# Softmax shift rows with the logarithm of the row sum in an attention and feed-forward kernel

## The reference

```
def xattn(q, k, v, wq, wk, wv, wo_w, wo_b):      # q = layernorm(x), k = v = ctx
    qp = rope(q @ wq.T); kp = rope(k @ wk.T); vp = v @ wv.T
    ...                                          # 16 heads of 32 features, blocks of 128 queries
    scores = (qh @ kband.T) * sqrt(32)           # keys at a distance of at most 128, others masked
    attn = softmax(scores)
    return (attn @ vband) @ wo_w.T + wo_b
x = x + xattn(layernorm(x), ctx, ctx, ...)
x = x + ffn(layernorm(x), ...)                   # 512 -> 2048 -> gelu -> 512, int8 weights, 16-bit activations
```

## Time and profile before

| What | Value |
|---|---|
| median of 3 runs | 1174.8 us (1173.72 to 1175.84) |
| the profiled execution's own time | 1176.49 us |
| its span | 1174.8 us |
| busy share: TensorE, VectorE, ScalarE, GpSimd | 97%, 81%, 55%, 32% |
| mean granted clock of TensorE | 0.988 |

### The profile page before, as it was taken

The page is one execution under the profiler, slowest core; times in us unless marked ns, Lnnn a source line. Parts: engine busy times, 40 slices in busy tenths (PEclk is TensorE's granted clock), DMA queues, the critical chain, the costliest instruction groups (busy, mean ns, idle before and its releaser), DMA issues.

```text
span 1174.8 us, 23540 instructions
## 1 busy us (share of the span) xinstructions
PE 1135.5 (97%) x7928; PEld 766.9 (65%) x7928; DVE 946.8 (81%) x2413; ACT 646.8 (55%) x1033; POOL 375.7 (32%) x540
## 2 busy tenths in 40 slices
PE   6999999999999999999999789999999999999998
PEld 6867887887788788778878464444444444444443
DVE  6879989999999999999998756666666687777776
ACT  5255356436534643563464255555555577777774
POOL 1247337534743663474365230000000021111121
PEclk9989999999999999999999799999999999999999
DMA  8554674566457556646753723555553402676662
GB/s 281 133 150 114 172 221 118 148 184 163 126 175 212 129 137 184 172 123 179 203 139 92 222 65 118 197 196 198 196 196 117 152 1 77 214 232 227 224 216 99
DMA packets 100522, 191.10 MB, mean 163 GB/s; under 512 B 13376, under 2 KB 30912, under 8 KB 100416
## 3 DMA queue, kind: packets, MB, share of 16 engines
q1 hardware_dynamic: 96096, 179.92, 50.9%
q10 hardware_dynamic: 4320, 9.83, 2.8%
HBM read 89.16 MB, written 43.91 MB: 113 GB/s over the span
## 4 chain that ended last, share of the span: by engine, by line
PE 44%; DVE 26%; issue 25%; DMA 2%; ACT 1%; SPq 1%; DVEq 0%; POOL 0%; POOLq 0%; ACTq 0%
PE bank L864 19%; DVE bank L1224 12%; PE bank L642 6%; PE bank L656 5%; PE bank L669 5%; DVE row_max L1224 3%; PE bank L589 3%; PE bank L593 2%; DVE neg_max L1265 2%; DVE roped L1250 2%; DVE rt L1248 2%; DVE rt L1247 1%; DVE neg_max L1229 1%; DVE t_lo L1257 1%; PE bank L608 1%
## 5 line engine op out<-in xcount | busy, mean ns | idle before, releaser
L1224 DVE CUSTOM_DVE_ANT_0 bank<-bank,mask 128x256 f32<-128x256 f32 x512 | 203.5, 453 | 33.9 <-PE bank L608 23.1
L864 PE MATMUL bank<-wout_int,g_hi 128*128 128x512 bf16 x512 | 193.6, 379 | 0.1
L864 PE MATMUL bank<-wout_int,g_lo 128*128 128x512 bf16 x512 | 193.6, 379 | 0.0
L825 PE MATMUL bank<-qT_hi,win_int 128*128 128x512 bf16 x496 | 188.0, 379 | 0.0
L825 PE MATMUL bank<-qT_lo,win_int 128*128 128x512 bf16 x496 | 188.0, 379 | 0.0
L973 ACT ACTIVATE probs<-bank 128x512 f32<-128x512 f32 x256 | 139.0, 599 | 37.0 <-PE bank L642 31.1
L1542 POOL TENSOR_TENSOR k_lo<-roped,k_hi 128x256 fp32r<-128x256 f32 x60 | 55.0, 947 | 263.5 <-ACT k_hi L913 263.5
L1520 DVE TENSOR_TENSOR g_lo<-h_int,g_hi 128x512 f16<-128x512 f32 x128 | 89.1, 696 | 41.3 <-ACT g_hi L1129 37.4
L1565 POOL TENSOR_SCALAR_AFFINE_SELECT probs<-probs 128x256 f32<-128x256 f32 x256 | 107.1, 429 | 35.9 <-ACT probs L973 30.0
L1097 ACT ACTIVATE h_ring<-bank,b_in,g_scale 128x512 f32<-128x512 f32 x96 | 73.1, 779 | 71.2 <-PE bank L825 56.4
L1462 DVE TENSOR_REDUCE hmax<-h_ring 128x512 f32 (+1 forms) x96 | 63.1, 682 | 58.5 <-ACT h_ring L1097 56.4
(11 more groups left out here) (170 smaller groups left out, 2735.0 us busy)
## 6 DMA issues: line engine op xcount, KB each, us to landing
hidden_scratch<-h_ring SPq DMA_DIRECT2D x96, 256.0 KB, 2.1
h_ring<-hidden_scratch SPq DMA_DIRECT2D x96, 256.0 KB, 2.9
k_st<-k_hi SPq DMA_DIRECT2D x128, 128.0 KB, 2.9
q_st<-q_hi SPq DMA_DIRECT2D x128, 128.0 KB, 2.7
xq<-x_scratch SPq DMA_DIRECT2D x16, 1024.0 KB, 6.0
x_ln<-in_x SPq DMA_DIRECT2D x16, 512.0 KB, 6.3
ctx_raw<-in_ctxT SPq DMA_DIRECT2D x16, 512.0 KB, 5.0
k_st<-k_lo SPq DMA_DIRECT2D x64, 128.0 KB, 2.8
```

Source lines behind the costliest of these rows:

```text
L825: mm = pe.matmul(bank[f % 4][:], win_int[:, c, f * P:(f + 1) * P], part[:, par, c], start=c == 0 and part is qT_hi, stop=c == KC - 1 and p ...
L864: return pe.matmul(bank[4 * par + u][:], part[:, f % 4, u * P:(u + 1) * P], wout_int[:, f], start=f == 0 and part is g_hi, stop=f == FC - ...
L1224: dve.tensor_tensor_reduce(sc, sc, mask[:, (1 - qb) * P:(1 - qb) * P + S], 1.0, NEG, ALU.add, ALU.max, row_max[:, qb, n:n + 1]).then_inc(m ...
```

## The change

The mask is now 0 or the largest float, the queries' weights are scaled by minus the square root of 32, and VectorE takes row minima of the negated scores (`row_minima`, same two passes). Then ScalarE takes exp(minimum - score) of each half in place in PSUM with `accum_out`, which gives the row sum (`row_sums`, 32 instructions a block). A bank of `ring` is released by ScalarE (`sum_done`) and no longer by VectorE. When all heads are through, `logs` takes the logarithm of the sums and exp of minus that; VectorE's `log_sums` makes of it, in five small chained operations, the shift row (logarithm minus minimum, with one correction step), in two parts. With this row the second set of exponentials is already divided by the sum. So `denominators`, `invert`, `store_sums`, `spread_shares`, `normalise`, `last_shares` and the two constant tables are gone. The transposed row is in bank 6 where it was in bank 7. ScalarE's copies of the first part are placed between its row sums (`xt_lead` behind head 3, `v_copy` behind 8, `split_hi` of the keys behind 9, `ot_lead` behind 12), `ctx_hi` moves behind exponential 4, and GpSimd's four `ctx_lo` move behind the bands of heads 10 to 13. The counts of output products become 12 ahead of the transposes, 4 behind them and 8 among the heads.

```diff
             def scores(b, n):
...
-                    pe.wait_ge(max_done, 2 * (H * b + n - 1))
+                    pe.wait_ge(sum_done, 2 * (H * b + n - 1))
...
             def clump(b, par, i, has_proj):
                 for kb in range(2):
-                    weighted(b, par, i, kb)
-                for kb in range(2):
-                    denominators(b, i, kb, has_proj)
+                    weighted(b, par, i, kb, has_proj)
...
-                some(7)
+                some(12)
                 max_transposes(b, has_proj)
                 some(4)
-                for n, count in enumerate((1, 2, 2, 2, 1, 1, 1, 0, 1, 1, 0, 0, 1, 0, 0, 0)):
+                for n, count in enumerate((1, 1, 1, 1, 1, 0, 1, 0, 1, 0, 0, 0, 1, 0, 0, 0)):
...
+            def row_sums(b, n):
+                if n == 0:
+                    wait(act, lse_chain, LSE_OPS * b)
+                act.wait_ge(min_done, 2 * (H * b + n + 1))
+                for qb in range(2):
+                    sc = ring[n % 2][:, qb * S:(qb + 1) * S]
+                    act.activation(sc, sc, ACT.Exp, scale=-1.0, bias=row_min[:, qb, n:n + 1],
+                                   accum_out=row_sum[:, qb, n:n + 1]).then_inc(sum_done, 1)
+
+            def logs(b):
+                act.wait_ge(sum_done, 2 * H * (b + 1))
+                act.activation(lse[:], row_sum[:], ACT.Ln).then_inc(log_done, 1)
+                act.wait_ge(log_done, 2 * b + 1)
+                act.activation(lse_e[:], lse[:], ACT.Exp, scale=-1.0).then_inc(log_done, 1)
...
             def step(b, par, has_c, has_o, has_proj, has_xt):
                 if has_proj:
                     norm1(b + 1)
-                if has_proj:
-                    xt_lead(b + 1, 0)
-                    xt_lead(b + 1, 1)
-                if has_o:
-                    store_sums(b - 1)
-                    spread_shares(b - 1)
-                if has_proj:
-                    v_copy(b + 1, 1 - par, 0)
-                    split_hi("k", b + 1)
-                if has_o:
-                    ot_lead(b - 1, 0, has_proj)
-                    ot_lead(b - 1, 1, has_proj)
+                for n in range(H):
+                    row_sums(b, n)
+                    if n == 3 and has_proj:
+                        xt_lead(b + 1, 0)
+                        xt_lead(b + 1, 1)
+                    if n == 8 and has_proj:
+                        v_copy(b + 1, 1 - par, 0)
+                    if n == 9 and has_proj:
+                        split_hi("k", b + 1)
+                    if n == 12 and has_o:
+                        ot_lead(b - 1, 0, has_proj)
+                        ot_lead(b - 1, 1, has_proj)
+                logs(b)
                 if has_proj:
                     v_copy(b + 1, 1 - par, 1)
-                if has_xt:
-                    ctx_hi(b + 2)
...
                 for n in range(H):
                     softmax_exp(b, n)
+                    if n == 4 and has_xt:
+                        ctx_hi(b + 2)
...
+            def log_sums(b):
+                hi, lo = shift[:, :, MROW:MROW + H], shift[:, :, MROW + H:P]
+                link = chain(dve, lse_chain, LSE_OPS * b)
+                dve.wait_ge(log_done, 2 * b + 1)
+                link(dve.tensor_tensor(lse_z[:], lse[:], row_min[:], ALU.subtract))
+                dve.wait_ge(log_done, 2 * b + 2)
+                link(dve.tensor_tensor(lse_t[:], row_sum[:], lse_e[:], ALU.mult))
+                link(dve.scalar_tensor_tensor(out=lse_z[:], in0=lse_t[:], scalar=-1.0, in1=lse_z[:], op0=ALU.add, op1=ALU.add))
+                link(dve.tensor_copy(hi.bitcast(F32R), lse_z[:]))
+                link(dve.tensor_tensor(lo.bitcast(F32R), lse_z[:], hi, ALU.subtract))
...
-                    between[0] += [lambda: invert(b - 1)]
-                    between[4] += [lambda: normalise(b - 1, 0), lambda: normalise(b - 1, 1)]
...
-                if has_xt:
-                    ctx_lo(b + 2, 0)
-                    ctx_lo(b + 2, 1)
                 for n in range(H):
                     band(b, n)
                     if 6 <= n < 10 and has_proj:
                         split_lo("q", b + 1, n - 6)
-                    if n in (1, 3) and has_xt:
-                        ctx_lo(b + 2, n // 2 + 2)
+                    if 10 <= n < 14 and has_xt:
+                        ctx_lo(b + 2, n - 10)
```

More of the change, by code:

```diff
@@ L40 @@
 SLOTS = 8
-HOT = DK + NC4 - 1
 FC = FF // P
@@ L74, in constants @@
     q, k = np.arange(S)[:, None], np.arange(S)[None, :]
-    mask = folded(folded(np.where(np.abs(q - k) <= WINDOW, 0.0, NEG).astype(np.float32), 0), 1)
+    mask = folded(folded(np.where(np.abs(q - k) <= WINDOW, 0.0, FAR).astype(np.float32), 0), 1)
     assert not mask[:P, :P].any() and not mask[P:, P:].any()
     mask = np.concatenate([mask[P:], mask[:P, P:]], 1)
-    hot = np.tile((np.arange(HOT) % NC4 == NC4 - 1).astype(np.float32), (P, 1))
-    row, col = np.arange(P)[:, None], np.arange(P)[None, :]
-    pick = np.stack([row == DK * (col // DK) + i for i in range(NC4)], 1).astype(np.float32)
     sel = np.zeros((P, H), np.float32)
@@ L761, in _ @@
             steps(pe, step)
-            def last_shares():
-                pe.wait_ge(pick_in, 16)
-                pe.wait_ge(exp_done, H * NB)
-                for s in range(2):
-                    pe.wait_ge(den_done, NB + s)
-                    for i in range(NC4):
-                        mm = pe.matmul(ring[s][:, i * P:(i + 1) * P], pick[:, i], den_r[:, s * P:(s + 1) * P],
-                                       start=True, stop=True)
-                    mm.then_inc(share_mm, 1)
             def last_products():
@@ L945, in ot_lead @@
             def ot_lead(j, s, has_q):
-                act.wait_ge(onorm, 2 * (j + 1) if j < NB - 1 else 2 * j + s + 1)
+                act.wait_ge(oT_out, 2 * (j + 1))
+                if s == 0:
+                    wait(act, o_mm, 2 * j)
                 if s == 0 and has_q:
@@ L1261, in xt_rest @@
                 rest(x_bank, s, xt_hi, 2 * j + s + 1, xt_lo)
-            def invert(b):
-                dve.wait_ge(den_mm, NC4 * (b + 1))
-                dve.reciprocal(den_r, den_bank[:, 0:S]).then_inc(den_done, 1)
-            def normalise(b, half):
-                dve.wait_ge(oT_out, 2 * b + half + 1)
-                dve.wait_ge(share_in, 16 * (b + 1))
-                part = oT[:, 2 * half:2 * half + 2].rearrange("p i t -> p (i t)")
-                dve.tensor_tensor(part, part, share[:, 2 * half * S:2 * (half + 1) * S], ALU.mult).then_inc(onorm, 1)
             def quantise_win(b):
@@ L1351, in step @@
                             work()
-                split_max(b)
+                log_sums(b)
                 if not has_proj:
```

120 lines of the change are left out of this document (43 added, 77 removed).

## The result

The changed kernel took 1327.1 us (median of 4 runs, 1321.97 to 1329.87) where the kernel before took 1175.3: a ratio of 1.129 (95% interval 1.125 to 1.133). The prediction was 1330. The profiled execution took 1321.97 us, the shortest of the four, with a span of 1320.3, at a mean granted clock of 0.951 (0.988 before).

The account below looks back on a forecast made before the run. TensorE's queue was taken to bound the attention part, ScalarE being half free. First part +8.8 us and second +1.3 made +10.2 a period, +153 for 15 blocks, +5 and -3: 1330 us, range 1260 to 1370.

Parts of the forecast that it names:

- The sum: Whole kernel: period 51.0 us against 40.8; +153 us for 15 blocks, +5 for the last, -3 behind it.
- the walk: Attention part, three engine queues followed in time: first part 33.1 us (+8.8), second 17.9 (+1.3).
- 0.60 us for a half: First part, one ScalarE row sum: 0.41 us exponential and 0.19 us accumulator read; bounds 0.47 to 0.63.
- The rival of the clock: Attention part: TensorE's clock falls after idle stretches, 5 us at 0.6 per block; up to +30 us, 1360; chance 0.08.
- its lower case, 1288: Whole kernel: same walk with row sum 0.47 us and copy 0.19 us; period 48.2 us, time 1288.
- the forecast case: Whole kernel: the walk's 51.0 us period, 1330 us, with no fall of the clock; chance 0.70.
- The signs: Expected in the profile: period near 51 us, TensorE idle 25%, late minima 4, GpSimd full from band 6 to 15.
- the lap of a bank: First part: scores now wait for VectorE and 1.2 us of ScalarE; a bank's lap goes from 1.67 to 2.92 us.
- Rival A: Attention part: ScalarE's content, not the laps, sets a period of 41.8 us; +15 us, 1190; chance 0.10.
- The copy to float32r: Shift row on VectorE: this copy taken as 0.6 us, between 0.19 and 1.07.
- The second part: Block's second part: GpSimd is last, with all four ctx_lo on its end; 17.9 us against 16.55, +1.3 us.
- 3.44 us per block, 55 us, if nothing else takes the time: TensorE's denominator products removed: 4 clumps x 0.86 us per block, 55 us over 16 blocks.

Follow-up runs that it names:

- experiment 7: Changed kernel without accum_out, sums left at 1 so outputs undivided; 1300.0 us (ratio 1.105 to 1.109).
- Experiment 1: Changed kernel plus 24 and 32 dummy identity products where TensorE waits for GpSimd's bands ahead of a block's last two groups of value products; 1291.8 us (1.100).
- experiment 3: Changed kernel with minima written to SBUF and banks released by VectorE: 1317.6 us; the same with ctx_hi and ctx_lo at their old places: 1248.1 us.
- edit 2: ctx_hi and the four ctx_lo back at the places of the kernel before; alone on the changed kernel 1275.3 us (1.085).
- experiment 6: e5 with row sums for the first half of the queries only, the others' outputs undivided; 1206.0 us (1.025 to 1.030).
- experiment 4: Changed kernel with edit 2, no row sums or logarithms, bank released by VectorE, shift row the negated minimum, outputs undivided; 1157.9 us (0.982 to 0.989).
- e7: The kernel of experiment 4: edit 2 on the changed kernel, without row sums and logarithms; 1157.9 us (0.982 to 0.989).
- e5: Changed kernel with minima into SBUF, banks released by VectorE, and edit 2; 1248.1 us (1.060 to 1.068).
- e3: Changed kernel with edit 2 alone, context parts back at their old places; 1275.3 us (1.085, 1.083 to 1.088).
- e4: Changed kernel with minima into SBUF and banks released by VectorE, context parts still late; 1317.6 us (1.119 to 1.124).
- experiments 8: quantise_win moved to the first part, behind head 9: on e3 1261.8 us, on e5 1251.0 us; the latter with 8 and 16 dummy products 1253.2 us.

## Why the prediction was right, and where two errors met

**The sum.** Expected +153 for 15 blocks, +5 for the last, -3 behind it. The shift rows of the profile stand at 64.37 and, 14 blocks on, at 776.88; before, `split_max` at 60.15 and 632.38. That is +4.2 in the first block and +140.3 in the 14 (a mean of 50.9 a block for 40.9; 51.2 where it is steady); the last block gives +5.4 and what is behind it -4.6: +145.3, the difference of the spans within 0.2 us. The steady period, 51.2, is the 51.0 of the walk. For this execution, the shortest of the four, the forecast was 1331.5, 9.5 us more than it took; the medians are 3 us apart.

**Two terms were wrong by as much, with opposite signs.** "0.60 us for a half" was too dear. The activation was 0.45 us as a record, where I had 0.52 from a full-width exponential and a bias; the read was 0.21, as bounded; but the read overlaps both its neighbours, where I took 0.11 out once and let the read stand nearly whole. By experiment 7 the activation alone is 0.38 us (told: 0.41) and the read adds 0.08 (told: 0.19): the read is the term that was mis-sized. 0.453 is below my lower bound, 0.47. The rival of the clock, at 0.08, came true on top of the forecast and in every steady block. Experiment 1 sets the two apart: with the clock held up, the second part is 17.9 us, the walk's very number, and the first 30.7 instead of 33.1. So the first part was overpriced by 2.4 us a block and the clock took 2.6. That the 2.4 us are the row sum's is worked out and not run apart: the walk itself gives as much for 0.13 us less a half, its lower case, 1288, and experiment 1 measured 1291.8. That the sum came out within 3 us is luck: had the clock held, as the forecast case had it, 1330 would have stood 38 us above the measured time. For that rival the prediction had noted what speaks for it, the fall behind 3.14 of 5 us in the earlier trace rows; here TensorE was busy 1.41 of 4.70 us before the fall. I had set 2.2 us as the longest gap, and so it was (2.13), but 1.64 us of idle time stand a little ahead of it. The Trainium skill (TensorE: Matmul & The Clock Gate, Part 1) says that the clock follows how busy TensorE was; the two windows agree with it.

**The signs.** Of what the prediction had named, the period, the cause of the idle time, minima 4, GpSimd's full queue from band 6 on and the feed-forward part came out. TensorE's idle time didn't: 17% of the steady period (busy 42.6 of 51.2 us) and not 25%, in part because its products took longer at the lower clock.

**The first part.** Its order was as told: late start of the row sums (2.45 us after scores 0, 2.7 told), `xt_rest` waiting for `xt_lead`, minima 4 at 10.5 (9.95 told; scores 2 come at 5.35 behind the low clock instead of 4.05), row sums 15 ended at 30.5 (31.25 told). But "the lap of a bank" isn't the one cause that the walk makes of it: take the laps away and 9.5 us go, none of them in the steady period and with the clock falling once more (experiment 3), or 27 with edit 2 made. ScalarE's work in the first part ends in nearly the same place. Rival A (ScalarE's content alone, 1190) had the right engine and the wrong price: it let ScalarE's work spread over a whole period, where the row sums can only stand between the first minima and the shift row.

**The copy to float32r.** I took 0.6 us for it, for fear of GpSimd. It took 0.18, but the first operation of the row, which I took as short, 0.73 us (timeline of the kernel after):

```profile
367.19 0.73 DVE L1209 TENSOR_TENSOR lse_z<-lse,row_min 128x32 f32<-128x32 f32 x1 [1.35 <-ACT lse L960]
...
368.40 0.18 DVE L1213 CAST shift<-lse_z 128x32 fp32r<-128x32 f32 x1
```
```profile
366.58 1.29 POOL L1524 TENSOR_TENSOR x_res<-x_res,wo_b 128x512 f32<-128x512 f32 x1
```

It ends at 367.92, GpSimd's operation at 367.87. The sum is nearly right (1.96 us from the end of row sums 15 to the transposes, 1.85 told) and its reason was not: it isn't the kind of operation that counts here, but which one meets GpSimd. The Trainium skill (SBUF — State Buffer, SBUF: two separate sides) also gives the wider rule, that a VectorE operation with two SBUF inputs is blocked by a GpSimd operation that reads SBUF. The first operation here, and the three with two inputs in experiment 6, agree. The fourth there is the cast, the one-source kind that the prediction had named.

**The second part.** Right in cause and size: GpSimd's four `ctx_lo` at the end. Put back, they give 52 us, not the 20 that the prediction put on the second part: 2.5 us a block there, which takes it below that of the kernel before, and 0.9 in the first part, where the lower clock ends sooner. These overlap with experiment 1's 2.6 us and can't be added to them.

**The removal.** "3.44 us per block, 55 us, if nothing else takes the time" was the step least tested, and something takes it: 16 us with everything else out (experiment 4). VectorE was busy 15.14 of the second part's 16.55 us; that was the next bound, one row away. Even the shortest steady periods of that experiment are only 1.6 us shorter than before; in nine of 14 periods VectorE's operation that waits for GpSimd takes 1.3 of them back, and in two the clock takes more than all. The walk didn't lean on the 55, since it priced the second part by GpSimd.

**The balance.** By runs: 1158 for e7, that is 16 less than before for the removals, + 90 for the row sums themselves (e7 to e5), + 27 for having them hold the bank (e5 to e3), + 52 for the late context parts and part of the clock's fall (e3 to the kernel after) is 1327. Another order of the edits gives other shares (the bank alone, from the kernel after, is 9.5). What the 90 us consist of beyond the number of pieces isn't settled; the shift row's longer chain is in it, and the clock differs too (0.980 in e7, 0.967 in e5).

## What to carry to other kernels

An engine with half of its time free isn't free at each moment: work put on it costs little only where it need not be done by a certain time, and here all of it stood between the first minima and one shift row. Before counting the time of removed work as a gain, look for the engine that is next: its busy time in the same window limits the gain. And a gap that another engine opens in TensorE's queue can be paid twice, once as idle time and again in the clock behind it. Look at every block before reading a cause from one: in experiment 4 blocks of one kernel differ by 3.5 us.

## What the runs showed of the hardware

An accumulating exponential of 128x256 from PSUM with a pointer bias costs 0.453 us, its read included (0.45 and 0.21 us as records), and 0.377 without the read (experiment 7). In SBUF the activation's record is 0.50 us (e4). VectorE's small SBUF operations, two-input ones and a cast, lasted until GpSimd's current operation ended: 0.19 us became 1.2 (experiment 6), and a one-source operation of 128x512 went from 0.49 to 3.2 us across one part of q and six bands (experiments 8 and 4). After TensorE had been busy 1.41 of 4.70 us the clock stood at the lower level for some 6.4 of the next 7.4 us, though TensorE was full in them. After a wait of 2.74 us it was at that level for most of the next 3.5 (experiment 3). After waits of 0.85 and 1.30 us it fell in one block and held in the next (experiment 4).
